# Copying a ring of per-tile LayerNorm statistics to its table in halves of eight tiles instead of wholes of sixteen

## What is computed

```python
x = x + L0_xattn(_layernorm(x), ctx, ctx, ...)      # softmax attention, 16 heads, 128 keys
x = x + L0_ffn(_layernorm(x), ...)                  # quantised: scale = max over the WHOLE tensor / 255
x = x + L1_xattn(_layernorm(x), ctx, ctx, mask, ...) # attention without softmax
x = x + L1_ffn(_layernorm(x), ...)
```

## Time and profile before

| what | us |
|---|---|
| median of 3 runs | 2006.84 (2006.36 to 2008.04) |
| the profiled execution, its own time | 2011.76 |
| its span, first to last instruction | 2010.0 |
| PE busy | 1871.1 (93%) |
| DVE busy | 1583.9 (79%) |
| ACT busy | 1232.9 (61%) |
| POOL busy | 952.4 (47%) |

### The profile page before, as it was taken

One profiled execution on the slowest core, in us unless ns is written; L12 is line 12 of the kernel. 1 busy time (PEld: TensorE's weight loads), 2 busy tenths in 40 slices (PEclk: granted clock), 3 DMA queues, 4 the chain that ended last, 5 costly groups with the idle time before them and its releaser, 6 DMA issues. The chain is left out here.

```text
span 2010.0 us, 30847 instructions
## 1 busy us (share of the span) xinstructions
PE 1871.1 (93%) x9191; PEld 1364.4 (68%) x9274; DVE 1583.9 (79%) x3612; ACT 1232.9 (61%) x3387; POOL 952.4 (47%) x1053
## 2 busy tenths in 40 slices
PE   6698789999999999999986999988999999999997
PEld 5576577877777778777863444446767767767775
DVE  6846578888887888888765888887888888888884
ACT  3434588888787878888862333235655555555543
POOL 2210355555555555555551000025666666666664
PEclk9799799999999999999998999999999999999999
DMA  8346101222223212321117999825445445444310
GB/s 276 122 136 220 48 32 58 71 77 64 64 69 81 64 61 63 78 64 43 42 50 274 391 353 363 317 108 205 147 157 185 156 159 186 159 159 159 139 53 38
DMA packets 124680, 276.03 MB, mean 137 GB/s; under 512 B 41056, under 2 KB 51296, under 8 KB 106208
## 3 DMA queue, kind: packets, MB, share of 16 engines
q1 hardware_dynamic: 121680, 272.69, 39.6%
q10 hardware_dynamic: 2832, 1.32, 0.3%
HBM read 165.95 MB, written 108.00 MB: 136 GB/s over the span
## 5 line engine op out<-in xcount | busy, mean ns | idle before, releaser
L1095 POOL TENSOR_TENSOR a_pr<-a_pr,a_rcp 128x512 f32<-128x512 f32 x256 | 266.5, 1041 | 348.5 <-DVE a_rcp L948 348.5
L871 ACT ACTIVATE a_pr<-a_s,a_nmax 128x128 f32<-128x128 f32 x1024 | 361.6, 368 | 64.4 <-DVE a_nmax L941 62.3
L1322 PE MATMUL f_pair<-f_room,w 128*128 128x512 bf16 x999 | 226.2, 383 | 11.8 <-DVE hmax L1549 9.2
L941 DVE TENSOR_REDUCE a_nmax<-a_s 128x4 f32<-128x512 f32 x256 | 175.6, 686 | 56.7 <-PE a_s L60 52.9
L871 ACT ACTIVATION_READ_ACCUMULATOR a_pr<-a_s,a_nmax 128x1 f32 x1024 | 211.0, 206 | 0.0
L1549 DVE CUSTOM_DVE_ANT_0 f_hf<-f_pair,nb,sh 128x512 f32<-128x512 f32 x248 | 175.0, 748 | 39.7 <-PE f_pair L1322 25.6
L956 DVE TENSOR_TENSOR a_pTl<-a_pt,a_pTh 128x512 fp32r<-128x512 f32 x256 | 175.3, 685 | 37.4 <-ACT a_pTh L880 37.4
L1769 POOL TENSOR_TENSOR f_ring<-f_ring,f_room 128x512 f32<-128x512 f32 x64 | 82.1, 1282 | 256.0 <-DVE f_room L1710 256.0
L1322 PEld LDWEIGHTS f_pair<-f_room,w 128*128 128x128 bf16 x1024 | 99.6, 99 | 126.7 <-DVE hmax L1549 9.7
L880 ACT ACTIVATE a_pTh<-a_pt 128x512 fp32r<-128x512 f32 x256 | 156.0, 609 | 29.9 <-PE a_pt L784 29.9
L784 PE MATMUL a_pt<-ident,a_pr 128*128 128x128 f32 x1024 | 157.2, 276 | 16.4 <-POOL a_pr L1095 8.7
(11 more groups left out here) (398 smaller groups left out, 5245.4 us busy)
## 6 DMA issues: line engine op xcount, KB each, us to landing
hidden<-f_hf SPq DMA_DIRECT2D x58, 1024.0 KB, 7.1
f_hf<-hidden SPq DMA_DIRECT2D x58, 1024.0 KB, 5.2
xb<-x SPq DMA_DIRECT2D x16, 1024.0 KB, 5.4
a_xr<-x SPq DMA_DIRECT2D x64, 256.0 KB, 3.6
x<-a_xr SPq DMA_DIRECT2D x64, 256.0 KB, 2.1
f_ring<-x SPq DMA_DIRECT2D x64, 256.0 KB, 4.8
out<-f_ring SPq DMA_DIRECT2D x64, 256.0 KB, 4.5
f_room<-x SPq DMA_DIRECT2D x15, 1024.0 KB, 9.7
```

Source lines behind the costliest of these rows:

```text
L871: last = e.activation(pr[:, t, j, :], s_bank[t][:, j * P:j * P + P], ACT.Exp, bias=nmax[kk % 2][:, t, j:j + 1], accum_out=sums[kk % 2][:, ...
L941: e.tensor_reduce(nmax[kk % 2][:, t, :], s_bank[t][:].rearrange("p (j n) -> p j n", j=4), AX, ALU.max, negate=True).then_inc(*e_max)
L1095: e.tensor_tensor(p, p, rcp[kk % 2][:, t, :].unsqueeze(2).to_broadcast([P, 4, KEYS]), ALU.mult).then_inc(*e_pn)
L1322: last = e.matmul(h_bank[(PAIRS * u + i) % 3][:, q, :], w1[:, k, f * P:f * P + P], xT[u % 2][:, k, :], start=k == 0, stop=k == KC - 1)
```

## The change

`keep` copies half a ring, eight columns, at a time, and is called at other steps. In `x1` it is called where o % 8 == 2, that is in steps 0 and 8 of the batches 1 to 3 and in step 16 of batch 3 (o = kk - 6), for the eight tiles whose last statistics were taken three steps before. The wait on `e_mk` that protects the ring now stands at o % 8 == 0 and looks at the half that is to be overwritten. The call after the last step copies the last eight tiles.

```diff
+        HALF = TPB // 2
@@ x1
-                if o % TPB == 0 and there(b, o - 1):
-                    keep(b, o - TPB)
-                    e_mk.wait_ge(e, b + o // TPB - 1)
+                if o % HALF == 0 and there(b, o - TPB):
+                    e_mk.wait_ge(e, b * 2 + o // HALF - 2)
+                if o % HALF == 2 and there(b, o - 2 - HALF):
+                    keep(b, o - 2 - HALF)
@@ keep
-                at = b * TPB + off
-                e_st1.wait_ge(e, at + TPB - 1)
-                e.tensor_copy(scr["mean1"][:, bass.ds(at, TPB)], mvb[:, :, 0])
-                e_r1.wait_ge(e, at + TPB - 1)
-                e.tensor_copy(scr["rstd1"][:, bass.ds(at, TPB)], rsb[:])
-                e.tensor_copy(scr["mx1"][:, bass.ds(at, TPB)], mxb[:]).then_inc(*e_mk)
+                at, s = b * TPB + off, slice(off % TPB, off % TPB + HALF)
+                e_st1.wait_ge(e, at + HALF - 1)
+                e.tensor_copy(scr["mean1"][:, bass.ds(at, HALF)], mvb[:, s, 0])
+                e_r1.wait_ge(e, at + HALF - 1)
+                e.tensor_copy(scr["rstd1"][:, bass.ds(at, HALF)], rsb[:, s])
+                e.tensor_copy(scr["mx1"][:, bass.ds(at, HALF)], mxb[:, s]).then_inc(*e_mk)
@@ after the last step
-            keep(NB - 1, 0)
+            keep(NB - 1, HALF)
```

## The result

The kernel after takes 1999.03 us in the median (1998.41 to 2000.07), the kernel before beside it 2006.84 (2006.16 to 2010.43). The ratio is 0.9963, 95% interval 0.9952 to 0.9973: faster by 5 to 10 us; the medians differ by 7.8. The profiled execution of after took 1999.01 us, its span is 1997.1 us.

A forecast was written before the change was run, and what follows sets the result against it. Attention was taken to run at PE's pace (busy 78.95 of 80.00 us). Removing three stalls, -7.89 us, plus 0.5 for a late GpSimd gave -7.4: 1999.4 us in the median, range 1997.2 to 2005.3.

The forecast's parts named there:

- the chain of the stall: Step 6: VectorE's `rsb` copy waits 1.68 us for GpSimd's power, then lasts 1.16 us beside `xbo`; PE idles 1.92 us.
- What the stalls cost, 7.89 us: PE's extra time in steps 6 and 7 of batches 1 to 3: 2.98, 2.80 and 2.11 us, booked as gain.
- The waits at the new place: At the later keep, statistics are three steps old and the power two, so neither wait can hold.
- The copies, 0.27 us, hidden: Each of seven keeps in steps moves `x1` by 3 x 0.09 = 0.27 us, at no cost on PE.
- The covers that I had named, at `smax` and at `plo`: Step 8: 0.54 us of cover at the second `smax`, 0.60 us idle before the next `plo`; both exceed 0.27.
- GpSimd made late, 0.5 us: Behind `rc`, copies getting in first delay `prob` by 0.07 us per keep: 0.5 us over seven, ends 0 and 1.3.
- What moves with the code, 1 us either way: Allowance of 1 us either way for the gap at the branch and the clock's dips.
- The lost race: Rival, chance 0.2: a copy finds `prob` running and waits; PE loses 0.8 us in six keeps, 2003.7 us.
- The slower rival: Rival, chance 0.08: keep copies lose race after race, each keep costing 2.6 us as now, giving 2017 us.

## Why the prediction was right, and where its steps were not

I had forecast 1999.4 us from a gain of 7.4; it came out at 1999.03 with a gain of 7.8. Step by step:

- **What bounds the kernel, and the chain of the stall.** Right. Later copies end the stall, smaller ones don't (the halves at the old place). GpSimd's hold on the copy is shown by moving `xbo` away: 0.17 for 1.16 us. In the Trainium skill, the page "SBUF — State Buffer", section "Who interferes with whom", has the whole-instruction lock; the trace agrees in the kernels with six copies and with the keep behind `smax`, where a held copy ends with GpSimd's instruction. It does not agree to the last tenth of a microsecond on who starts first: a copy that began 0.03 us after the record of GpSimd's `prob` was still let through, in all seven keeps with four copies.
- **What the stalls cost, 7.89 us.** The stretches were measured rightly, but I took the chance of one execution for a price. This is the term that was off. Without a low clock a stall costs 2.0 to 2.1 us, 6.3 in all; each low clock adds about 0.9. The execution that I read had two, the second trace of before one (7.2 us). I had seen that batch 3 was cheaper because its clock stayed at 1.00, and left the dips in the sum all the same. The gain of the medians, 6.5 and 7.8 us, is what one or two low clocks would make of it, but the unprofiled executions have no trace, so how many they had is not shown.
- **The waits at the new place.** Right: neither holds. Half the distance would have done.
- **The copies, 0.27 us, hidden.** They move `x1` by 0.22 us, and the steps with one cost 0.02 us. The covers that I had named, at `smax` and at `plo`, held; the second shrank from 0.60 to 0.37.
- **GpSimd made late, 0.5 us.** Mis-sized: it is 0. I had spaced all copies by the first one's 0.09 us and so put the third at 0.27, behind `prob`; the later ones follow at 0.05 and 0.07, and the third starts at 0.21. With a fourth copy the term exists, at 0.03 us in steps 8 and 9.
- **What moves with the code, 1 us either way.** Something moved: 0.7 us are lost at step 15, in both traces of after. I had looked for it at the branch alone, and the 0.3 us won there are no more than two executions of before differ by. The 0.7 stand where the 0.5 for GpSimd had stood, so the sum is right partly by an exchange of two errors.

That the number came out within half a microsecond is partly luck. The same account without any low clock gives 6.3 - 0.7 = 5.6 us, and 7.9 - 0.7 = 7.2 with the two low clocks of the execution that I had read. Both are estimates from these traces.

**The rivals.** The lost race didn't happen, and it was less near than I had feared: the last copy starts 0.04 us ahead of `prob`, and a fourth one 0.03 us behind it still got in. Where the race was forced, it cost 0.6 us a keep, not 0.8, and 2002.9 us in place of 2003.7. The slower rival's way, with VectorE losing one turn after another, never showed: exactly one copy lost in each of the seven keeps with six copies. Its price was too high too. With every keep at the full stall the halves give 2014.6 us, not 2017.

**What stays open.** Why the granted clock falls behind one idle time of 1.92 us and not behind another. The same question stands behind tile 0, which comes at 290 to 291 us in most traces and near 295 in the first of before and the one with eight memsets: these two have a low clock twice more in the lead-in. Here is the first such place in before, then the same stretch of work in its second trace, whose tile 0 comes at 290.60 us:

```profile
217.70:228.51 10.81, 8.58 (x26) 6.25 (x26) 3.54 (x8) 5.04 (x23) 1.66 (x2) 0.68 0.43 130
...
216.62:224.69 8.07, 5.71 (x26) 4.16 (x26) 3.64 (x8) 5.03 (x23) 1.80 (x2) 1.00 0.53 162
```

The times of single executions go the same way: of eleven of before, the fastest (2001.60 us) had a mean granted clock of 0.981, the two slowest (2011.33 and 2011.67) 0.974 and 0.973. And that the gap of 0.30 us is VectorE waiting for its code is argued from its wandering, not shown: no row shows a fetch.

## What to carry to other kernels

A copy out of a ring should stand a tile later than the last thing that is written to it; the distance costs nothing if the ring has room, while the same copy one step too early cost 2 us each time. Put small VectorE copies where GpSimd is idle, and count how long it will be: three fitted into 0.25 us, a fourth just got in, and of six one was always held, for about 1 us. When an engine has slack on average but one step of four is over its measure, divide the large portion before changing the order: the order gave nothing, the division 6 us. And when a cost is read from one execution, look at its granted clock, and whether a second execution has it in the same place.

## What the runs showed of the hardware

- The low clock comes in some executions and not in others. PE idle for 1.92 us at the same instruction of the same kernel was followed by 3.5 us at 0.54 in one execution and at 1.00 in another, and after waited 2.29 us behind the branch without a low clock. With the clock near its lower level of 1.2 GHz, in place of 2.4, for those 3.5 us a stall cost 0.9 us more.
- A copy of 8 columns lasts 0.14 to 0.17 us, and such copies follow each other at 0.05 to 0.07 us. Which of them a GpSimd instruction of 128x512 holds is decided about 0.1 us behind the start of its record. Copies that began 0.03 to 0.04 us after it were let through in 13 of 14 keeps (the kernels with four and with six copies), those at about 0.10 us in three of six, those at 0.14 us or more in none. A copy that got in so late made GpSimd's instruction longer: 1.10 us after four copies, 1.19 to 1.20 after five, in place of 1.04. Three copies beside GpSimd's power of 128x1, from 0.11 us behind its start, were not held (one keep). Which copy of a row of six lost varied from keep to keep (the fourth once, the fifth and sixth three times each).
- Straight code on VectorE has gaps of 0.30 us that belong to its position: at step 15 in both traces of after and in the kernels with the keep behind `smax` and with `vsum` first, at step 8 in the kernels with the keep at multiples of eight and one tile later, and nowhere visible with eight instructions ahead of the body, with four or six copies, with the normalisation split, or in before and the kernel with `xbo` later. The gap behind the branch was 2.9 to 3.4 us over the kernels, but 3.29 and 2.95 in two executions of before. The Trainium skill, page "Runtime: NRT & Kernel Launch", section "Instruction fetch mechanics", says that code comes in blocks of 256 instructions, whose boundary is mostly hidden, and that a taken branch out of the loaded blocks stops the engine for a fetch. That the gap of 0.30 us wanders with the position agrees; no run here shows the fetch itself.
